# The last residual addition of a fused decoder layer moves from VectorE to GpSimd, in front of the sum into x2

## The reference, cut to what matters

```python
x = x + _L0_attn_ref(_layernorm(x), ...)            # RWKV-like mixing, 32 heads, chunks of 64
x = x + _L0_xattn_ref(_layernorm(x), ctx_512, ctx_512)   # 32 query heads, 8 kv heads
x = x + _L0_ffn_ref(_layernorm(x), ...)             # MXINT8 fake-quantised MLP

# in _L0_ffn_ref:
x = bf16_round(inputs); residual = bf16_round(inputs)
h = mx_layernorm(x, ln_w, ln_b)
h = mx_linear(h, W1, b1)            # quantise, 512 -> 2048, round to bf16
h = mx_gelu(h)
h = mx_linear(h, W2, b2)            # quantise, 2048 -> 512, round to bf16
return bf16_round(residual + h)     # the addition that this change moves
```

## Time and profile before

| | us |
|---|---|
| median of 3 runs | 1299.24 (1298.41 to 1301.25) |
| the profiled execution, its own time | 1299.69 |
| its span, first to last instruction | 1297.9 |
| PE busy | 1225.6 (94%) |
| DVE busy | 1096.3 (84%) |
| ACT busy | 813.4 (63%) |
| POOL busy | 643.9 (50%) |
| mean granted TensorE clock | 0.989 of full speed |

### The profile page before, as it was taken

One profiled execution on the slowest core, in us unless ns is written; L12 is line 12 of the kernel. 1 busy time (PEld: TensorE's weight loads), 2 busy tenths in 40 slices (PEclk: granted clock), 3 DMA queues, 4 the chain that ended last, 5 costly groups with the idle time before them and its releaser, 6 DMA issues.

```text
span 1297.9 us, 34513 instructions
## 1 busy us (share of the span) xinstructions
PE 1225.6 (94%) x13318; PEld 791.9 (61%) x13352; DVE 1096.3 (84%) x1912; ACT 813.4 (63%) x1580; POOL 643.9 (50%) x703
## 2 busy tenths in 40 slices
PE   5789999999999999999999999999999999999864
PEld 4566666566666666667666666666666666566421
DVE  7898988997888878888888988888898888878875
ACT  4566756566666666666667666666776665576541
POOL 7866355555455444544543454454446545454323
PEclk9999999999999999999999999999999999999987
DMA  8655132322223221222222113122212223312222
GB/s 293 164 151 149 37 78 61 68 53 61 65 69 73 73 65 35 61 73 62 65 73 72 36 49 86 54 73 73 73 42 55 53 62 73 85 48 44 70 53 61
DMA packets 137330, 97.08 MB, mean 75 GB/s; under 512 B 108112, under 2 KB 110160, under 8 KB 136400
## 3 DMA queue, kind: packets, MB, share of 16 engines
q1 hardware_dynamic: 137168, 94.87, 28.9%
HBM read 37.16 MB, written 8.39 MB: 35 GB/s over the span
## 4 chain that ended last, share of the span: by engine, by line
PE 81%; DVE 6%; issue 4%; DMA 3%; ACT 3%; SPq 1%; POOL 1%; POOLq 0%; ACTq 0%; DVEq 0%
PE bank_b L746 16%; PE bank_a L746 8%; PE bank_y L800 8%; PE bank_a L736 7%; PE bank_y L864 6%; PE rt L815 5%; PE rt L828 5%; PE rt L765 4%; PE bank_o L834 4%; PE bank_b L855 4%; PE bank_a L855 4%; PE bank_o L792 2%; PE bank_y L784 2%; PE bank_y L779 1%; PE bank_o L846 1%
## 5 line engine op out<-in xcount | busy, mean ns | idle before, releaser
L5012 POOL TENSOR_TENSOR gmem<-gmem,unit_g 128x1024 bf16<-128x1024 bf16 x64 | 126.3, 1974 | 242.9 <-DVE unit_g L2094 242.9
L2041 DVE TENSOR_REDUCE negm<-rt 128x16 f32<-128x2048 f32 x64 | 146.4, 2288 | 12.3 <-PE rt L815 11.6
L3735 ACT ACTIVATE pT<-rt 128x2048 f32<-128x2048 f32 x64 | 120.0, 1875 | 41.3 <-PE rt L828 24.9
L800 PE MATMUL bank_y<-w_Wo,yT 128*128 128x512 f32 x256 | 117.8, 604 | 5.3 <-issue 3.2
L864 PE MATMUL bank_y<-w2q,gmem 128*128 128x512 bf16 x478 | 113.0, 385 | 9.2 <-DMA gmem<-gmem 6.0
L746 PE MATMUL bank_a<-mix_r,w_Wr 128*128 128x128 f32 x1024 | 121.5, 277 | 0.1
L746 PEld LDWEIGHTS bank_b<-mix_k,w_Wk 128*128 128x128 f32 x1024 | 118.6, 193 | 4.4 <-issue 4.4
L746 PEld LDWEIGHTS bank_a<-mix_r,w_Wr 128*128 128x128 f32 x1024 | 117.2, 192 | 6.4 <-issue 5.3
L746 PE MATMUL bank_b<-mix_g,w_Wg 128*128 128x128 f32 x1024 | 120.1, 276 | 0.0
L746 PE MATMUL bank_b<-mix_k,w_Wk 128*128 128x128 f32 x1024 | 119.8, 275 | 0.0
L746 PEld LDWEIGHTS bank_b<-mix_g,w_Wg 128*128 128x128 f32 x1024 | 117.4, 192 | 2.2 <-issue 1.0
(11 more groups left out here) (262 smaller groups left out, 2831.5 us busy)
## 6 DMA issues: line engine op xcount, KB each, us to landing
qx<-qdense SPq DMA_DIRECT2D x64, 224.0 KB, 3.3
context<-ctx SPq DMA_DIRECT2D x32, 384.0 KB, 3.7
xin<-x SPq DMA_DIRECT2D x32, 256.0 KB, 3.5
gmem<-w SPq DMA_DIRECT2D x16, 512.0 KB, 4.6
out<-x SPq DMA_DIRECT2D x32, 256.0 KB, 2.4
vp<-vz SPq DMA_DIRECT2D x32, 128.0 KB, 3.5
odense<-oT SPq DMA_DIRECT2D x128, 32.0 KB, 2.0
pT<-Wv SPq DMA_DIRECT2D x1, 1024.0 KB, 8.9
```

The source lines that it names most:

```text
L800: done = e.matmul(bank_y[:, :], yT[:, c, :], wt["Wo"][:, c, :], start=(c == 0), stop=(c == KT - 1))
L2041: e.tensor_reduce(negm[:, 0:H].rearrange("p (g a j) -> p g j a", g=4, a=2)[:, :, 2 * i:2 * i + 2, :], rt[:, :].rearrange("p (g j a s) -> p ...
L3735: e.activation(pT[:, :, :].rearrange("p g n -> p (g n)"), rt[:, :], ACT.Exp, scale=float(D) ** -0.5).then_inc(sem(f"act_ex{i}"), 1)
L5012: e.tensor_tensor(blocks(half), blocks(half), per_block(unit[f"g{i}"], 32), ALU.mult).then_inc(sem(f"pool_gsc{i}"), 1)
```

## The change

The residual leaves VectorE's queue for all 32 sequences. It becomes the first of two GpSimd instructions of `last_sum(n)`, with a semaphore wait between them. Both now count on the same semaphore, `pool_y`, so every wait for a last sum is for an even count, and the wait of `normalise_f(n)` for the residual of n - 2 is for the odd count 2n - 3. In GpSimd's written order, 21 of the 32 calls of `last_sum` stand at another place, all of them earlier, most by one to three helpers and the first two by more; the other 11 (n = 4 to 7, 9, 13, 26 and 28 to 31) stay. Besides this, TensorE waits in front of its first `scores_r` for the second count of `act_Wv` (the copy of bv_row, L3785) too.

```diff
             def store(n):
-                e.wait_ge(sem("pool_y"), n + 1)
+                e.wait_ge(sem("pool_y"), 2 * n + 2)
...
             project_v(0)
+            e.wait_ge(sem("act_Wv"), 2)
             scores_r(0, 0)
...
             def second_out(n):
                 e.wait_ge(sem("pe_down1"), n + 1)
                 if n:
-                    e.wait_ge(sem("dve_res"), n)
-                    e.wait_ge(sem("pool_y"), n)
+                    e.wait_ge(sem("pool_y"), 2 * n)
...
-            def residual(n):
-                e.wait_ge(sem("dve_o"), n + 1)
-                if n:
-                    e.wait_ge(sem("pool_y"), n)
-                e.tensor_tensor(o_bf, a_bf[n % 2][:, :], o_bf, ALU.add).then_inc(sem("dve_res"), 1)
...
             second_out(2)
             normalise_o(4)
-            residual(2)
             gelu_round(3, 0)
...
             norm_mv("f", 28)
-            residual(26)
             stats_g(28)
...
             gelu_pow2(28, 1)
-            residual(27)
             e.wait_ge(sem("pe_Xo1"), 30)
...
-            residual(30)
             second_out(31)
-            residual(31)
...
             def normalise_f(n):
                 e.wait_ge(sem("act_rs_f"), 3 * n + 3)
                 if n >= 2:
-                    e.wait_ge(sem("dve_res"), n - 1)
+                    e.wait_ge(sem("pool_y"), 2 * n - 3)
...
             def last_sum(n):
-                e.wait_ge(sem("dve_res"), n + 1)
+                e.wait_ge(sem("dve_o"), n + 1)
+                e.tensor_tensor(o_bf, a_bf[n % 2][:, :], o_bf, ALU.add).then_inc(sem("pool_y"), 1)
+                e.wait_ge(sem("pool_y"), 2 * n + 1)
                 e.tensor_tensor(x2[n % 3][:, :], x2[n % 3][:, :], o_bf, ALU.add).then_inc(sem("pool_y"), 1)
...
             gelu_scale(3, 0)
+            last_sum(2)
             second_sum(4)
-            last_sum(2)
             gate_parts(6)
...
             second_sum(21)
+            last_sum(19)
             gate_parts(23)
             mixed(24, "g")
-            last_sum(19)
...
             gelu_scale(28, 0)
+            last_sum(27)
             gelu_scale(28, 1)
-            last_sum(27)
             gate_parts(31)
...
```

More of the change, by code:

```diff
@@ L2354, in _ @@
             differences(5)
-            residual(0)
             normalise_o(2)
@@ L2402, in _ @@
             gelu_max(2, 1)
-            residual(1)
             stats_f(3)
@@ L2488, in _ @@
             second_out(3)
-            residual(3)
             norm_mv("f", 5)
@@ L2524, in _ @@
             differences(9)
-            residual(4)
             maxima(7, 1)
@@ L2573, in _ @@
             mixed(10, "k")
-            residual(5)
             stats_f(7)
@@ L2618, in _ @@
             mixed(11, "k")
-            residual(6)
             gate(10)
@@ L2659, in _ @@
             gelu_max(8, 1)
-            residual(7)
             maxima(10, 0)
@@ L2699, in _ @@
             up_out(9, 2, bank_a)
-            residual(8)
             maxima(11, 0)
@@ L2742, in _ @@
             second_out(9)
-            residual(9)
             maxima(12, 0)
@@ L2787, in _ @@
             maxima(13, 0)
-            residual(10)
             gate(14)
@@ L2832, in _ @@
             gelu_round(12, 0)
-            residual(11)
             stats_f(13)
@@ L2876, in _ @@
             gate(16)
-            residual(12)
             stats_f(14)
@@ L2918, in _ @@
             gelu_round(14, 0)
-            residual(13)
             stats_f(15)
@@ L2962, in _ @@
             gelu_round(15, 0)
-            residual(14)
             norm_mv("f", 16)
@@ L3005, in _ @@
             gelu_round(16, 0)
-            residual(15)
             norm_mv("f", 17)
@@ L3047, in _ @@
             second_out(16)
-            residual(16)
             stats_f(18)
@@ L3088, in _ @@
             maxima(20, 0)
-            residual(17)
             gate(21)
@@ L3133, in _ @@
             gate(22)
-            residual(18)
             stats_f(20)
@@ L3176, in _ @@
             gate(23)
-            residual(19)
             stats_f(21)
@@ L3219, in _ @@
             stats_f(22)
-            residual(20)
             gelu_round(21, 0)
@@ L3262, in _ @@
             normalise_o(23)
-            residual(21)
             stats_f(23)
@@ L3305, in _ @@
             gelu_max(23, 1)
-            residual(22)
             e.wait_ge(sem("pe_Xo1"), 25)
@@ L3354, in _ @@
             gelu_round(24, 0)
-            residual(23)
             gate(27)
@@ L3391, in _ @@
             stats_f(26)
-            residual(24)
             norm_mv("f", 26)
@@ L3436, in _ @@
             decayed(29, 1)
-            residual(25)
             mixed(30, "k")
@@ L3549, in _ @@
             up_out(29, 3, bank_b)
-            residual(28)
             gelu_round(29, 0)
@@ L3568, in _ @@
             second_out(29)
-            residual(29)
             denominators(31)
@@ L5101, in _ @@
             gelu_scale(1, 0)
+            last_sum(0)
             mixed(5, "r")
@@ L5108, in _ @@
             gelu_scale(1, 1)
-            last_sum(0)
             mixed(6, "r")
@@ L5113, in _ @@
             second_sum(3)
+            last_sum(1)
             gelu_scale(2, 1)
@@ L5120, in _ @@
             mixed(7, "r")
-            last_sum(1)
             gelu_scale(3, 0)
+            last_sum(2)
             second_sum(4)
-            last_sum(2)
             gate_parts(6)
@@ L5134, in _ @@
             second_sum(5)
+            last_sum(3)
             gate_parts(7)
-            last_sum(3)
             gate_rstd(7)
@@ L5183, in _ @@
             second_sum(10)
+            last_sum(8)
             with_bias(13)
-            last_sum(8)
             mixed(13, "g")
@@ L5205, in _ @@
             mixed(15, "g")
+            last_sum(10)
             gate_parts(14)
             by_parity(15)
-            last_sum(10)
             gate_rstd(14)
@@ L5215, in _ @@
             gate_parts(15)
+            last_sum(11)
             mixed(16, "g")
-            last_sum(11)
             gate_rstd(15)
@@ L5225, in _ @@
             mixed(17, "g")
+            last_sum(12)
             gate_parts(16)
-            last_sum(12)
             gate_rstd(16)
@@ L5246, in _ @@
             gate_parts(18)
+            last_sum(14)
             by_parity(19)
-            last_sum(14)
             gate_rstd(18)
@@ L5256, in _ @@
             gate_parts(19)
+            last_sum(15)
             by_parity(20)
-            last_sum(15)
             gate_rstd(19)
@@ L5266, in _ @@
             gate_parts(20)
+            last_sum(16)
             by_parity(21)
-            last_sum(16)
             gate_rstd(20)
@@ L5275, in _ @@
             mixed(22, "g")
+            last_sum(17)
             gate_parts(21)
-            last_sum(17)
             gate_rstd(21)
@@ L5285, in _ @@
             mixed(23, "g")
+            last_sum(18)
             gate_parts(22)
             by_parity(23)
-            last_sum(18)
             gate_rstd(22)
@@ L5304, in _ @@
             mixed(25, "g")
+            last_sum(20)
             gate_parts(24)
-            last_sum(20)
             by_parity(25)
@@ L5311, in _ @@
             gelu_scale(22, 0)
+            last_sum(21)
             second_sum(23)
-            last_sum(21)
             with_bias(25)
@@ L5324, in _ @@
             second_sum(24)
+            last_sum(22)
             with_bias(27)
             gate_parts(26)
-            last_sum(22)
             gate_rstd(26)
@@ L5333, in _ @@
             mixed(28, "g")
+            last_sum(23)
             gate_parts(27)
@@ L5337, in _ @@
             by_parity(28)
-            last_sum(23)
             with_bias(28)
@@ L5344, in _ @@
             mixed(29, "g")
+            last_sum(24)
             gate_parts(28)
-            last_sum(24)
             gate_rstd(28)
@@ L5354, in _ @@
             second_sum(27)
+            last_sum(25)
             gate_parts(29)
-            last_sum(25)
             gate_rstd(29)
```

## The result

The changed kernel takes **1308.2 us** in the median of 4 runs (1305.78 to 1309.02), the kernel before 1299.7 on the same chip. The ratio is 1.0066, with a 95% interval of 1.0052 to 1.0080: slower by 8.5 us, where 1299.7 was forecast and 1302.9 was the end of the range. Measured once more, unaltered, on another chip (`after_again`), the ratio is 1.0072 (1.0051 to 1.0094).

What follows compares the result with a forecast made beforehand. TensorE was taken as the bound, busy 1029.99 of 1040 us from 160 to 1200. +0.7 + 0.4 - 0.6 = +0.5 us on 1299.69 gave 1300.2, as a median 1299.7, range 1296.3 to 1302.9.

Steps and rivals of the forecast that it cites:

- What is added: "Cost nothing": Middle stage: 32 GpSimd passes of 1.10 us, 35 us in all, fit GpSimd's idle time before gate_rstd; counted at nothing.
- The cover of 2.7 us: TensorE, 160 to 1200 us: only 2.7 us of waits hang on VectorE's chain; otherwise its work is covered.
- The first rule: A VectorE instruction with two SBUF inputs and a GpSimd instruction reading SBUF exclude each other for a whole instruction.
- Rival 2: Pass drawn out to 1.6 us, normalise_f waiting for it, at residual(26) and the end: +3.0, 1302.2 us; chance 0.16.
- last_sum's new places, at nothing or a gain: GpSimd's queue: earlier last_sum calls go into idle time, counted at nothing; last_sum(2) before second_sum(4) at -0.6 us.
- The end, +0.7: Behind second_out(31): GpSimd's residual pass and a wait start the very last sum later, +0.7 us.
- normalise_f(28), +0.4: ScalarE waits for residual(26) on GpSimd, starting 0.8 us later; half reaches up(28), +0.4 us, bounds 0 and 0.8.
- Sequence 2 to 4, -0.6: last_sum(2) before second_sum(4) lets stats_f(4) start earlier, which up(4) waited for: -0.6 us, bounds -0.9 and 0.
- VectorE's relief, 0: Middle stage: the 21.9 us removed from VectorE lie under TensorE's work and were counted at nothing.
- The clock, rival 3: Tail: a shift brings three matmul groups in or out of low clock, 0.83 us each: 1302.2 or 1297.2; chance 0.08.
- both slow rivals: The drawn-out GpSimd pass (chance 0.16) and the low clock's slow side (0.08 for both sides), each at 1302.2 us.
- GpSimd 35 us busier, VectorE 22 less or somewhat less: Expected sign in busy times if right: GpSimd about 35 us busier, VectorE about 22 us less or somewhat less.

Runs made afterwards that it cites:

- the reading one: Changed kernel without the residual; in its place one GpSimd addition of a 512-column bf16 scratch buffer to itself, nobody waiting for it: 1309.3 us, ratio 1.0061.
- e6: Changed kernel with last_sum at its old places except for tiles 0 and 1, and three buffers for a instead of two: 1308.8 us, ratio 1.0057.
- e1: Kernel before with only the change's new order of last_sum on GpSimd; the residual stays on VectorE: 1304.4 us, ratio 1.0027.
- the third buffer: Changed kernel with three buffers for a instead of two, its new order kept: 1310.1 us, ratio 1.0065.
- e2: Changed kernel with last_sum at its old places except for the first two tiles; residual on GpSimd, two buffers for a: 1325.05 us, ratio 1.0186.
- e12: Changed kernel with residuals of eleven tiles back on VectorE and these tiles' sums at their old places too: 1299.3 us, ratio 0.9989.
- e4: Changed kernel without the residual; in its place two GpSimd memsets of 600 bf16 columns, which only write: 1303.1 us, ratio 1.0020.

## Why the prediction was wrong, step by step

- *What is added: "Cost nothing".* This is the step that failed. It asked where GpSimd's extra 1.1 us would go in GpSimd's own queue and found the idle time in front of gate_rstd; that was so (109.7 us of it are left, of the 123.5 in the earlier trace rows). It did not ask what the pass does to the engine beside it, and the cover under TensorE's work that it counted on in the middle stage was not there: 5.9 us of idle time came to TensorE between 160 and 1200. The writing pass, which has that queue cost and hardly any other, is at +2.6 us; the reading one at +7.9.
- *The cover of 2.7 us.* I read the earlier trace rows as a bound on what VectorE's chain can do to TensorE. It bounds a gain, and not even that wholly: the row of 1.1 us for ScalarE's yT, which the earlier trace rows leaves out, hangs on VectorE too. Before the first of its two waits, at 729, ScalarE stood 2.12 us for VectorE's mv_g. What a longer chain costs is not in a list of the waits that are there: mix_k, vz and vp were not in it, because they came in time, and the trace has no row for how narrowly: mix_k, 1.9 us late at 1143, cost TensorE 1.5.
- *The first rule.* I quoted it, saw it confirmed in the earlier trace rows, and priced it as half a stretch, 0.93/2, once in the tail. Rows for more were there: the mean of the VectorE residual was 0.25 us above its undisturbed time. Rival 2 named the right mechanism at the wrong places (residual(26), the very end) and with 3.0 us for 8.5. That GpSimd reads twice in a row, right behind second_out, so that one VectorE instruction can meet both, was in none of the rivals.
- *last_sum's new places, at nothing or a gain.* The order alone costs 3.5 us (1.0012 to 1.0042). It also gains 0.5 to 0.6 us at 729 and at 767 us, where these two waits for yT stood, in every kernel with the new order; but `e6`, with the old places, has 0.3 and 0.5 there, so the order is not alone in it. The early sums beside mix_k and mix_v (0.5 us at 231, 0.2 at 1105, 0.9 at 1144 in `e1`) cost more.
- *The end, +0.7.* Right for the last pair (+0.77, pass 1.15 us for 1.10), but the pair of tile 30 in front of it was not looked at. With both back on VectorE 2 us return (1.0066 to 1.0050; the intervals overlap).
- *normalise_f(28), +0.4.* It waits 1.18 us for GpSimd, 0.8 more than before, as worked out; up(28) behind it is not later, so 0, the lower bound. The expected release by GpSimd was seen, and the third buffer gave nothing.
- *Sequence 2 to 4, -0.6.* Right in size, and by luck: stats_f(4) starts at 265.26, 1.2 us earlier than in the earlier trace rows, in a trace that runs 0.7 ahead there, and TensorE gains 0.5 us at 272. But up(4) still waits 0.84 us, and last_sum(2) in front of second_sum(4) is not the reason: with that order and the residual on VectorE (`e1`) nothing is gained at 272, with the old order and the residual on GpSimd (`e2`, `e6`) 0.5 us are. It is residual(2) leaving VectorE's queue, which the prediction had at nothing.
- *VectorE's relief, 0.* With the new order, leaving out the residual gains 3.3 us (1.0027 to 1.0002, intervals overlapping); `e12`, with 21 residuals off VectorE, is at -1.4 us, and zero is not excluded. So 0 may have been low, but that is not where the error was.
- *The clock, rival 3.* From 160 to 1200 us the granted clock is 1.00 before and after, so the loss there is not the clock's. In the tail the rival is real, but it goes with the execution: from 1249 to 1259 us the granted clock is 0.51 in `after` and 0.83 in `after_again`, the same kernel, and TensorE makes up 1.8 us there that `after` does not. From 1222 to 1225 `after` has 0.50 and the trace before 1.00; TensorE was busy throughout these 3 us. What this costs was not taken apart.
- *The range.* Its end of 1302.9 is 0.7 above both slow rivals (1302.2 each), and no row gives it.
- *GpSimd 35 us busier, VectorE 22 less or somewhat less.* GpSimd: 41 us. VectorE: 5 more. This one pair of numbers from the page after was the quickest sign that the cause is not in a queue.

## What to carry to other kernels

Before a pass over SBUF is moved to GpSimd, look at what VectorE does during it: every VectorE instruction with two SBUF inputs that overlaps it can be late by the whole pass (0.9 us here for 512 columns, 1.9 for two in a row), and idle time on GpSimd hides none of that. The passes that stand behind it on GpSimd move as well, onto other instructions. Waits that the trace lists bound what can be gained, not what can be lost; for a loss, ask by how little the producers of the other inputs were in time. And if an offload is made, make it for the tiles in which it draws out little: with 21 of 32 tiles moved nothing was lost, though nine of their pairs still draw VectorE out by 0.4 to 1.3 us; the other 11, with six early sums among them, made the whole loss. Which tiles these are was read from the trace after the change, not foreseen.

## What the runs showed of the hardware

- A bf16 pass of two inputs takes GpSimd as long as one with f32 output and one f32 input: 1.15 us for 512 columns in both (at 1301.62 and 1302.85). Half the bytes buy nothing.
- A GpSimd memset of 600 bf16 columns takes 0.60 us, and mix_k beside two of them 1.13 us, its undisturbed time.
- Two forms of VectorE instruction with one input are hit too, both a tensor_scalar on 16-bit types: gelu_round (bf16 to int16) went from 0.42 to 1.36 us, a 128x64 instruction on uint16 from 0.20 to 1.16. They are held up by memsets as well (0.78 and 0.63 us in `e4`), which the instructions with two inputs are not. One-input statistics stay at their time to 0.01 us, and so do maxima, which read PSUM. The same section of the Trainium skill has it that a tensor_scalar can enter a two-port mode and then contends; the trace agrees for gelu_round.
